# FFN of a cross-attention layer on one core: input and output products in one block with shared buffers, first operands of the output product loaded in the last step

## The chip, the cores and the metric

One core of a Trainium2 chip. The metric is the device time of the whole program in microseconds (us), the median of several executions.

## The reference

The layer is a cross-attention with a residual, followed by an FFN with a residual. `x` is [16, 112, 1024] float32, so there are 1792 tokens of width 1024. The part at issue is the FFN, cut here to what matters (`w1`, `w3` [3584, 1024], `w2` [1024, 3584] come as quantized values with one scale per 128x128 block; the quantization of the activations is undone at once and changes only rounding):

```
x = x + attention(layernorm(x), ctx)
h = silu(layernorm(x) @ w1.T) * (layernorm(x) @ w3.T)     # [1792, 3584]
out = x + h @ w2.T                                        # [1792, 1024]
```

## The kernel before

The program runs four stages, each a function of its own with its own `nc.Block()`: `queries`, `attention`, `mixing` (output projection, residual, second layer norm, transposed activations), `gate_up` (the two input products of the FFN) and `down` (the output product). At the end of a block all engines meet, and the buffers that a stage opened are given back. `stash` (12 x 1024 floats on each of 128 partitions) is the one buffer that outlives the stages.

Every float32 matrix product is made of three matmuls on operands split in a high part (rounded to `float32r`, made by ScalarE as a copy) and a low part (the rest, made by VectorE as `source - high` in `to_lo`, L90): high x high, high x low, low x high (L84, L85, L86 in `split_product`). Both FFN products are done by a Strassen-like scheme with 7 block products in place of 8.

**`gate_up`.** 56 steps `mi` (2 token halves x 28: 14 pairs of 128 hidden rows, `w1` and `w3` in turn). A step has 7 products `i` of 4 x 3 matmuls of 448 columns, counted by semaphore `prod`. ScalarE and VectorE split the next step's weights (`split_w`) while TensorE multiplies. VectorE adds the products (`add`, L1462), then forms `h = silu * up` in four blocks (`hidden`, L1467, in odd steps at i = 4, 5, 6: two at i = 4). GpSimd then forms four sums of the h blocks (`hidden_sums`, L1266 to L1274), and SyncE stores three h blocks and four sums (`store_h`, L1205, L1209) to `h_scr` in HBM. During the second half of the steps the kernel also prepares `w2`: VectorE transposes it (L1418), GpSimd forms four combinations (`down_sums`, L1282 to L1290), SyncE stores 3 + 4 blocks (`store_w2`, L1225, L1229) to `b_scr`. In the last step, mi = 55, the transposes of the last pair of `w2` are done at i = 0 to 3; there is nothing left to split for a next step. After the loop SyncE issues `store_w2(13)` and `store_h(27)`, and the block ends.

**`down`.** 49 tiles n = 7 i + t (7 block products i, 7 token tiles t of 128 tokens), each 14 x 3 matmuls of 512 columns into bank n % 8. The A operand (h, 128 x 1792 floats per tile, 896 KB) is loaded per tile into one of two slots, waits for its slot's split and is split whole (`AH`, `AL`). The B operand (w2, 14 pieces of 128 x 512 per i) is loaded in two halves of 7 pieces (1792 KB each) into one buffer of 7, and split piece by piece into a ring of 21. SyncE's queue in `down` is, in order: B half 0, A tile 0, B half 1, A tile 1, then the residual `y` (all 7 MB of it, 16 DMAs, L1637), then for each n: A tile n + 2, a B half at t = 0 and t = 6, and the stores of finished output tiles. VectorE's first output tile waits for the whole of `y`. VectorE and ScalarE do 7 B splits, then A tile 0, then the 7 other B splits, before they come to A tile 1. TensorE waits for A's low part at each tile, and in tile t = 0 for each piece of B.

The buffers of `down` are `y` [128, 2, 7, 1024], the rings `BH`, `BL`, and `AH`, `AL`; those of `gate_up` are `XH`, `XL`, `WH`, `WL`, `xT`, `t1`, `su`, `Sh`. They stand in the same memory one after the other, so nothing of `down` can be loaded before `gate_up` has ended, except into `stash`.

Of the kernel before, what the change touches and what calls it, by code (L numbers as in the profile page):

```python
# [21 lines left out]
def build_program(nc, x, ctx, wq, wk, wv, wo, w1, w1_scale, w3, w3_scale, w2, w2_scale, out):  # L22
# [7 lines left out]
    P = 128  # L30
    B, SQ, D = x.shape
# [26 lines left out]
    FB = 512  # L58
# [38 lines left out]
    with top:  # L97
# [1017 lines left out]
        def gate_up(xT):  # L1115
            with ExitStack() as st:
# [60 lines left out]
                def hcols(g):  # L1177
                    return slice(g * TB, (g + 1) * TB)

                with nc.Block() as block:  # L1180
                    @block.sync
                    def _(sp):
# [54 lines left out]
                        for mi in range(2 * NM):  # L1237
# [63 lines left out]
                    def _(act):  # L1301
# [63 lines left out]
                        for mi in range(2 * NM):  # L1365
                            P_, nxt = mi // 2, mi + 1 < 2 * NM
                            for i in range(7):
# [20 lines left out]
                                if i == 5 and mi >= NM and mi % 2 == 0:  # L1388
                                    scale_raw2((mi - NM) // 2)

                    @block.vector
                    def _(dve):
# [95 lines left out]
                        for mi in range(2 * NM):  # L1488
                            P_, up, nxt = mi // 2, mi % 2 == 1, mi + 1 < 2 * NM
                            for i in range(7):  # L1490
# [37 lines left out]
                                if i < 4 and mi >= NM and up:  # L1528
                                    make_w2T((mi - NM) // 2, i)

# [28 lines left out]

        def down():  # L1560
            with ExitStack() as st:
                def sb(name, shape, dt=f32):
                    return st.enter_context(nc.sbuf_tensor("d_" + name, shape, dt))

                def s_(name):
                    return sem("d_" + name)
                RING, HP = NP + NP // 2, NP // 2
                y = sb("y", [P, 2, MT, D])
                V = stash[:, 4:8, :].rearrange("p a (c n) -> p (a c) n", n=FB)
                BH, BL_ = sb("BH", [P, RING, FB], f32r), sb("BL", [P, RING, FB], f32r)  # L1570
                AH, AL = sb("AH", [P, 2, NP, P], f32r), sb("AL", [P, 2, NP, P], f32r)
                a_in = stash[:, 8:12, :].rearrange("p (e a) (c n) -> p e (a c) n", e=2, n=P)[:, :, 0:NP, :]
                b_in = stash[:, 0:4, :].rearrange("p a (c n) -> p (a c) n", n=FB)
                y_loaded = s_("y_loaded")
                a_loaded_ = [s_("a_loaded0"), s_("a_loaded1")]
                b_loaded = s_("b_loaded")
                a_hi, a_lo, b_hi, b_lo = s_("a_hi"), s_("a_lo"), s_("b_hi"), s_("b_lo")
                done, freed = s_("done"), s_("freed")
                v_done, c_done, out_ = s_("v_done"), s_("c_done"), s_("out")
                y_stored = s_("y_stored")  # L1580
                N = 7 * MT

                def part(r, c, t):
                    return y[:, r, t, c * FB:(c + 1) * FB]

                def rows(r, t):

                    out_rows, m = [], t * P
                    while m < (t + 1) * P:
                        n = min((t + 1) * P, (m // TB + 1) * TB) - m  # L1590
                        out_rows.append((m - t * P, n, m // TB * HALF + r * TB + m % TB))
                        m += n
                    return out_rows

                FINAL = {2: (0, 0), 4: (1, 1), 5: (1, 0), 6: (0, 1)}

                def ring(i, p):
                    return (NP * i + p) % RING

                with nc.Block() as block:  # L1600
                    @block.sync
                    def _(sp):
                        def load_b(i, h):

                            k = 2 * i + h
                            wait(sp, b_lo, HP * k)
                            sp.dma_start(b_in[:, 0:HP, :], b_scr[i, :, h * HP:(h + 1) * HP, :]
                                         ).then_inc(b_loaded, 16)

                        def load_a(n):  # L1610
                            i, t = n // MT, n % MT
                            wait(sp, a_lo, n - 1)
                            sp.dma_start(a_in[:, n % 2, :, :], h_scr[i, :, :, t * P:(t + 1) * P]
                                         ).then_inc(a_loaded_[n % 2], 16)

                        def store(i, t):
                            r, c = FINAL[i]
                            sp.wait_ge(out_, MT * sorted(FINAL).index(i) + t + 1)
                            for at, n, tok in rows(r, t):
                                sp.dma_start(of[tok:tok + n, c * FB:(c + 1) * FB],  # L1620
                                             part(r, c, t)[at:at + n, :]).then_inc(y_stored, 16)
                        of = out.rearrange("b q n -> (b q) n")
                        sp.wait_ge(b_stored, 112 * NP)
                        load_b(0, 0)
                        for stored in h_stored:
                            sp.wait_ge(stored, 48 * NP)
                        load_a(0)
                        sp.wait_ge(sh_stored, 64 * 2 * NP)
                        load_b(0, 1)
                        load_a(1)  # L1630
                        for stored in res_stored:
                            sp.wait_ge(stored, 16 * NT_TOK // 2)
                        n_res = 0
                        for t in range(MT):
                            for r in range(2):
                                for at, n, tok in rows(r, t):
                                    sp.dma_start(y[at:at + n, r, t, :], y_scr[tok:tok + n, :]  # L1637
                                                 ).then_inc(y_loaded, 16)
                                    n_res += 1
                        for n in range(N):  # L1640
                            i, t = n // MT, n % MT
                            if n + 2 < N:
                                load_a(n + 2)
                            if t in (0, MT - 1) and i + 1 < 7:
                                load_b(i + 1, 0 if t == 0 else 1)
                            if n and (n - 1) // MT in FINAL:
                                store((n - 1) // MT, (n - 1) % MT)
                        store(6, MT - 1)
                        sp.wait_ge(y_stored, 16 * sum(len(rows(r, t)) for r in range(2)
                                                      for t in range(MT)) * 2)  # L1650

                    def splits(eng, split_a, split_b, out_tile):
# [4 lines left out]
                        for n in range(N):  # L1657
                            i, t = n // MT, n % MT
                            if n + 1 < N:
                                split_a(n + 1)  # L1660
# [125 lines left out]
```

## Time and profile before

| | |
|---|---|
| median of 3 runs | 2568.43 us (2562.58 to 2568.75) |
| profiled execution | 2569.67 us, span 2567.7 us, mean granted TensorE clock 0.972 |
| TensorE busy | 2429.3 us (95% of the span), 12682 matmuls |
| VectorE, ScalarE, GpSimd busy | 1694.4, 980.1, 555.0 us |
| DMA | 408.02 MB, mean 159 GB/s |

The span is the time from the first to the last instruction of the profiled execution. Matmuls are pipelined, so "busy" of TensorE counts overlapping pieces; what tells is where it stood still and at which clock it ran. The clock column of the windows is 1.00 for 2.4 GHz and 0.50 for 1.2 GHz. "SPq" is a DMA issued from SyncE's queue.

### The profile page before, as it was taken

What the parts mean: (1) busy time and instruction counts of PE and PEld (TensorE: products, weight loads), DVE (VectorE), ACT (ScalarE), POOL (GpSimd) and SP (SyncE); (2) the same over time, 40 slices, a digit from 0 to 9 for tenths busy, and PEclk for the clock granted to TensorE, in tenths of its full rate; (3) what the DMA queues carried; (4) which work ended last, traced back from release to release, by engine and by line L of the source; (5) the groups of instructions that cost most, each with busy time, mean ns of one, the idle gap of its engine ahead of it and who ended that gap; (6) DMA issues with size and microseconds to landing.
All of it is one profiled execution on the core that took longest, in us unless ns stands there. A gap on an engine that the chain in (4) does not pass through costs nothing. (4 is left out here: it accounts for less than half of the span.)

```text
span 2567.7 us, 35357 instructions
## 1 busy us (share of the span) xinstructions
PE 2429.3 (95%) x12682; PEld 2073.0 (81%) x12682; DVE 1694.4 (66%) x2639; ACT 980.1 (38%) x1673; POOL 555.0 (22%) x305
## 2 busy tenths in 40 slices
PE   7998999999998799599999998999999949999999
PEld 6987877877884488499999987989898938888887
DVE  6425777777776444788888888788888734445442
ACT  3212445444444321544444444443344322332231
POOL 1000445445445300011111111233332210000000
PEclk9998999999998899799999999999999979999999
DMA  7535555555535435375566553677666595455552
GB/s 227 171 88 146 140 134 138 146 132 140 149 88 133 114 125 170 90 221 163 162 181 182 157 173 86 195 206 202 181 175 178 182 312 164 150 181 158 176 155 86
DMA packets 365224, 408.02 MB, mean 159 GB/s; under 512 B 125360, under 2 KB 323632, under 8 KB 356000
## 3 DMA queue, kind: packets, MB, share of 16 engines
q1 hardware_dynamic: 365088, 406.21, 54.7%
q8 instruction: 85, 1.39, 0.2%
q14 instruction: 51, 0.42, 0.1%
HBM read 252.99 MB, written 152.70 MB: 158 GB/s over the span
## 5 line engine op out<-in xcount | busy, mean ns | idle before, releaser
L84 PE MATMUL bank<-g_XH,g_WH 128*128 128x448 f32 x1568 | 580.7, 370 | 44.2 <-DVE g_su L1462 22.5
L85 PE MATMUL bank<-g_XL,g_WH 128*128 128x448 f32 x1568 | 578.5, 369 | 0.0
L86 PE MATMUL bank<-g_XH,g_WL 128*128 128x448 f32 x1568 | 578.3, 369 | 0.0
L1326 ACT ACTIVATE g_WH<-stash 128x512 fp32r<-128x512 f32 x392 | 241.6, 627 | 427.5 <-PE bank L86 249.2
L84 PEld LDWEIGHTS bank<-g_XH,g_WH 128*128 128x128 f32 x1568 | 296.5, 189 | 78.8 <-DVE g_WL L90 49.2
L696 DVE TENSOR_REDUCE a_nm<-bank 112x1 f32<-112x375 f32 x512 | 265.1, 531 | 116.8 <-PE bank L831 113.2
L90 DVE TENSOR_TENSOR g_WL<-stash,g_WH 128x512 fp32r<-128x512 f32 x392 | 283.8, 727 | 58.8 <-ACT g_WH L1326 49.7
L86 PEld LDWEIGHTS bank<-g_XH,g_WL 128*128 128x128 f32 x1568 | 296.4, 189 | 28.0
L85 PEld LDWEIGHTS bank<-g_XL,g_WH 128*128 128x128 f32 x1568 | 296.6, 189 | 27.6
L84 PE MATMUL bank<-d_BH,d_AH 128*128 128x512 f32 x686 | 269.4, 393 | 34.0 <-DVE d_AL L90 34.0
L800 ACT ACTIVATE a_pr<-bank 125x448 f32<-125x448 f32 x384 | 204.8, 545 | 207.4 <-PE bank L907 152.8
L85 PE MATMUL bank<-d_BL,d_AH 128*128 128x512 f32 x686 | 268.9, 392 | 0.0
L86 PE MATMUL bank<-d_BH,d_AL 128*128 128x512 f32 x686 | 268.7, 392 | 0.0
L649 POOL TENSOR_TENSOR a_prsum<-a_pr 125x1792 f32<-125x1792 f32 x32 | 129.3, 4042 | 364.0 <-ACT a_pr L800 364.0
L1673 ACT ACTIVATE d_AH<-stash 128x1792 fp32r<-128x1792 f32 x49 | 83.5, 1704 | 314.8 <-PE bank L86 292.2
L1462 DVE TENSOR_TENSOR g_su<-bank,g_su 128x448 f32<-128x448 f32 x280 | 170.6, 609 | 36.0 <-PE bank L86 35.9
L831 PE MATMUL bank<-a_kst,a_qst 96*112 96x376 f32 x512 | 183.1, 367 | 5.6 <-DVE a_nm L696 2.6
L84 PEld LDWEIGHTS bank<-d_BH,d_AH 128*128 128x128 f32 x686 | 130.1, 190 | 61.8 <-DVE d_AL L90 34.8
L85 PEld LDWEIGHTS bank<-d_BL,d_AH 128*128 128x128 f32 x686 | 130.1, 190 | 27.2
L86 PEld LDWEIGHTS bank<-d_BH,d_AL 128*128 128x128 f32 x686 | 130.0, 189 | 27.2
L907 PE MATMUL bank<-a_qst,a_kst 98*125 98x448 f32 x384 | 147.7, 389 | 2.9 <-ACT a_pr L800 2.6
L831 PEld LDWEIGHTS bank<-a_kst,a_qst 96*112 96x112 f32 x512 | 91.7, 179 | 69.3 <-DVE a_nm L696 32.7
(132 smaller groups left out, 4181.5 us busy)
## 6 DMA issues: line engine op xcount, KB each, us to landing
stash<-h_scratch SPq DMA_DIRECT2D x49, 896.0 KB, 5.7
stash<-in_L_ffn_w SPq DMA_DIRECT2D x168, 256.0 KB, 5.1
weight_scratch<-stash SPq DMA_DIRECT2D x28, 1024.0 KB, 7.7
stash<-weight_scratch SPq DMA_DIRECT2D x28, 1024.0 KB, 7.4
h_scratch<-g_Sh SPq DMA_DIRECT2D x112, 224.0 KB, 3.4
down_scratch<-xT SPq DMA_DIRECT2D x98, 256.0 KB, 3.0
stash<-down_scratch SPq DMA_DIRECT2D x14, 1792.0 KB, 8.8
stash<-in_ctx SPq DMA_DIRECT2D x48, 500.0 KB
```

What stands on the lines that cost most here:

```text
L84: pe.matmul(acc, lh, rh, start=first, stop=False, skip_group_check=onto)
L85: pe.matmul(acc, lh, rl, start=False, stop=False, skip_group_check=onto)
L86: return pe.matmul(acc, ll, rh, start=False, stop=last, skip_group_check=onto)
L90: return nc.vector.tensor_tensor(dst, src, hi.bitcast(f32), ALU.subtract)
L649: pool.tensor_tensor(prsum[:], pr[0:CK, :, 0, :], pr[0:CK, :, 1, :], ALU.add).then_inc(two_added, 1)
L696: nc.vector.tensor_reduce(nm[:, 1 - par, h:h + 1], s_bank[h % 2][0:SQ, 0:SK], AX.X, ALU.max, negate=True).then_inc(max_done, 1)
L800: nc.scalar.activation(pr[0:CK, r, c, :], st_bank[u % 2][0:CK, 0:J * SQ], ACT.Exp, scale=SCALE).then_inc(exp_done, 1)
L831: pe.matmul(s_bank[h % 2][0:SQ, 0:SKP], qst[0:96, 1 - par, g, j * SQ:(j + 1) * SQ], kst[0:96, 1 - par, g, :], start=True, stop=True).then_ ...
L907: pe.matmul(st_bank[u % 2][0:CK, 0:J * SQ], kst[0:98, par, g * R + r, c * CK:(c + 1) * CK], qst[0:98, par, g * R + r, :], start=True, stop ...
L1326: nc.scalar.activation(WH[:, i, :, :], w_source(mi, i), ACT.Copy).then_inc(w_hi, 1)
L1462: nc.vector.tensor_tensor(su[:, slot, :], acc[mi % 2][:, 0:TB], su[:, other, :], ALU.add).then_inc(summed, 1)
L1673: nc.scalar.activation(AH[:, n % 2, :, :], a_in[:, n % 2, :, :], ACT.Copy).then_inc(a_hi, 1)
```

## The change

`gate_up` and `down` become one function `ffn` with one block. Each engine's program for the output product (`down_sync`, `down_scalar`, `down_vector`, `down_tensor`) follows its program for the input products without a meeting point.

- The operands of the output product get the memory of the input products: the B ring (now 24 pieces) lies in `XH`/`XL`, the A slots in `WH`/`WL`, A tiles are loaded into a part of `hb` (in `stash`) and into `t1`, B pieces into `stash` (for i = 0 into 14 slots that the raw weights, `wT` and `S` held; from i = 1 on in chunks of 4 into 4 slots), the residual of r = 0 into `xT`, that of r = 1 into 14 free half rows of `stash`, `Sh` and `su`.
- In the last step (mi = 55) SyncE waits for the stores of the h blocks up to P_ = 26 and issues A tile 0; when the last weight split is done, B pieces 0 to 6, A tile 1, B pieces 7 to 11. Then `store_w2(13)`, a wait for it, B pieces 12 and 13, two residual tiles, `store_h(27)`, a wait for all h stores, and the tiles of the output product.
- In the last step ScalarE and VectorE split A tile 0 and B pieces 0, 1 at i = 4, pieces 2 to 4 at i = 5, pieces 5 to 11 at i = 6, behind that step's own additions and h blocks; pieces 12 and 13 come after the loop, then A tile 1.
- The residual is loaded tile by tile, in two column halves (32 DMAs in place of 16): r = 0 two tiles ahead, r = 1 from n = 3 on, one tile per n. An output tile waits for its own residual tile alone.
- From i = 1 on a chunk of B is loaded at t = 0, 2, 4, 6, each when all pieces of the one before it are split; pieces are split in the order `NEXT_B`.

```
-                RING, HP = NP + NP // 2, NP // 2
-                y = sb("y", [P, 2, MT, D])
-                BH, BL_ = sb("BH", [P, RING, FB], f32r), sb("BL", [P, RING, FB], f32r)
-                AH, AL = sb("AH", [P, 2, NP, P], f32r), sb("AL", [P, 2, NP, P], f32r)
+                RING, HP = 24, NP // 2
+                flat = [x[:, :, :, :].rearrange("p a k n -> p (a k n)") for x in (XH, XL)]
+                BH, BL_ = (f[:, 0:RING * FB].rearrange("p (s n) -> p s n", n=FB) for f in flat)
...
+                unit = stash[:, 0:8, :].rearrange("p a (c n) -> p (a c) n", n=FB)
+                BC = 4
...
+                def load_b(sp, i, c):
+                    p0, p1 = c * BC, min((c + 1) * BC, NP)
+                    sp.wait_ge(b_lo, NP * i + p0 if c else NP * i)
+                    sp.dma_start(unit[:, 0:p1 - p0, :], b_scr[i, :, p0:p1, :]).then_inc(d_b_loaded, 16)
+                FIRST_LOADS = ((0, HP), (HP, NP - 2), (NP - 2, NP))
+                def load_first_b(sp, k):
+                    p0, p1 = FIRST_LOADS[k]
+                    sp.dma_start(unit[:, b_slot(0, p0):b_slot(0, p1 - 1) + 1, :], b_scr[0, :, p0:p1, :]
+                                 ).then_inc(d_b_first[k], 16)
+                def load_a(sp, n):
+                    i, t = n // MT, n % MT
+                    wait(sp, a_lo, n - 1)
+                    sp.dma_start(a_in[n % 2], h_scr[i, :, :, t * P:(t + 1) * P]
+                                 ).then_inc(d_a_loaded[n % 2], 16)
+                def load_y(sp, r, t):
+                    for at, n, tok in rows(r, t):
+                        for c in range(2):
+                            sp.dma_start(part(r, c, t)[at:at + n, :], y_scr[tok:tok + n, c * FB:(c + 1) * FB]
+                                         ).then_inc(d_y_loaded[r][t], 16)
+                def down_sync(sp):
...
+                    for n in range(N):
+                        i, t = n // MT, n % MT
+                        if n + 2 < N:
+                            load_a(sp, n + 2)
+                        if t % 2 == 0 and i + 1 < 7:
+                            load_b(sp, i + 1, t // 2)
+                        if i == 0 and t + 2 < MT:
+                            load_y(sp, 0, t + 2)
+                        if n == 3:
+                            sp.wait_ge(b_lo, NP)
+                        if 3 <= n < 3 + MT:
+                            load_y(sp, 1, n - 3)
+                        if n and (n - 1) // MT in FINAL:
+                            store((n - 1) // MT, (n - 1) % MT)
...
+                FIRST_B = [range(0, 2), range(2, 5), range(5, NP - 2)]
+                NEXT_B = [range(*c) for c in ((0, 0), (0, 2), (2, 4), (4, 6), (6, 8), (8, 10), (10, NP))]
...
+                    dve_split_b(0, range(NP - 2, NP))
+                    for n in range(N):
+                        i, t = n // MT, n % MT
+                        if n + 1 < N:
+                            dve_split_a(n + 1)
+                        if i + 1 < 7:
+                            dve_split_b(i + 1, NEXT_B[t])
+                        out_tile(n)
...
                 with nc.Block() as block:
                     @block.sync
...
+                            if mi == 2 * NM - 1:
+                                sp.wait_ge(h_stored[0], 48 * NP)
+                                sp.wait_ge(h_stored[1], 48 * (NP - 1))
+                                sp.wait_ge(sh_stored, 64 * (2 * NP - 1))
+                                load_a(sp, 0)
+                                sp.wait_ge(w_lo, 7 * 2 * NM)
+                                sp.wait_ge(S_made, 4 * 2 * NM)
+                                sp.wait_ge(b_stored, 112 * (NP - 1))
+                                load_first_b(sp, 0)
+                                load_a(sp, 1)
+                                load_first_b(sp, 1)
...
                         store_w2(NP - 1)
+                        sp.wait_ge(b_stored, 112 * NP)
+                        load_first_b(sp, 2)
+                        load_y(sp, 0, 0)
+                        load_y(sp, 0, 1)
                         store_h(2 * NP - 1)
+                        for stored in h_stored:
+                            sp.wait_ge(stored, 48 * NP)
+                        sp.wait_ge(sh_stored, 64 * 2 * NP)
+                        sp.wait_ge(prod, 7 * 2 * NM)
+                        down_sync(sp)
...
                     @block.vector
...
                                 if i < 4 and mi >= NM and up:
                                     make_w2T((mi - NM) // 2, i)
+                                if mi == 2 * NM - 1 and i >= 4:
+                                    if i == 4:
+                                        dve_split_a(0)
+                                    dve_split_b(0, FIRST_B[i - 4])
+                        down_vector()
```

## Rows read from the trace of the kernel before

**Rows 1.** The page: the span in 40 equal slices, busy tenths of TensorE.

```profile
PE   7998999999998799599999998999999949999999
```

**Rows 2.** Timeline of TensorE around the change of stage (start us, us, ..., idle before).

```profile
2058.08 0.37 PE L86 MATMUL bank<-g_XH,g_WL 128*128 128x448 f32 x1
...
2079.64 0.80 PE L84 MATMUL bank<-d_BH,d_AH 128*128 128x512 f32 x1 [21.19 <-DVE d_AL L90]
...
2114.47 0.80 PE L84 MATMUL bank<-d_BH,d_AH 128*128 128x512 f32 x1 [12.77 <-DVE d_AL L90]
```

**Rows 3.** The chain that ended last, in order of time (start us, us, what).

```profile
2065.10 7.08 DMA stash<-down_scratch
...
2091.37 19.27 DMA stash<-h_scratch
```

**Rows 4.** Windows of 2 us: length, busy of PE, PEld, DVE, ACT, POOL, then clock, DMA share, GB/s.

```profile
2060.00:2062.00 2.00, 0.00 (x0) 0.00 (x0) 0.00 (x0) 0.00 (x0) 1.92 (x2) 0.90 0.71 256
...
2084.00:2086.00 2.00, 2.00 (x7) 1.57 (x6) 1.15 (x2) 1.81 (x4) 0.00 (x0) 0.63 1.20 312
...
2088.00:2090.00 2.00, 2.00 (x11) 1.65 (x10) 1.59 (x3) 1.54 (x1) 0.00 (x0) 1.00 1.02 410
...
2096.00:2098.00 2.00, 2.00 (x11) 1.65 (x10) 0.00 (x0) 0.00 (x0) 0.00 (x0) 1.00 1.05 242
```

**Rows 5.** Timelines: VectorE's output tiles in the steady stage, and the last instruction.

```profile
2393.28 1.29 DVE L1710 TENSOR_TENSOR d_y<-bank,d_y 128x512 f32<-128x512 f32 x2 [4.49 <-PE bank L86]
...
2402.80 1.29 DVE L1710 TENSOR_TENSOR d_y<-bank,d_y 128x512 f32<-128x512 f32 x2 [5.10 <-PE bank L86]
...
2564.64 0.69 DVE L1710 TENSOR_TENSOR d_y<-bank,d_y 128x512 f32<-128x512 f32 x1 [8.83 <-PE bank L86]
```

**Rows 6.** Timeline of VectorE in the last step and at the start of `down`.

```profile
2044.12 0.69 DVE L90 TENSOR_TENSOR g_WL<-stash,g_WH 128x512 fp32r<-128x512 f32 x1 [2.37 <-ACT g_WH L1326]
...
2053.53 0.62 DVE L1467 TENSOR_TENSOR stash<-bank,stash 128x448 f32<-128x448 f32 x1 [1.24 <-PE bank L86]
2054.07 1.46 DVE L1467 TENSOR_TENSOR stash<-g_su,stash 128x448 f32<-128x448 f32 x1
...
2059.14 0.62 DVE L1467 TENSOR_TENSOR stash<-g_su,stash 128x448 f32<-128x448 f32 x1
2072.86 4.30 DVE L90 TENSOR_TENSOR d_BL<-stash,d_BH 128x512 fp32r<-128x512 f32 x7 [13.09 <-ACT d_BH L1685]
2077.56 2.02 DVE L90 TENSOR_TENSOR d_AL<-stash,d_AH 128x1792 fp32r<-128x1792 f32 x1 [0.40 <-ACT d_AH L1673]
```

**Rows 7.** Timeline of GpSimd in the same stretch.

```profile
2053.74 1.30 POOL L1285 TENSOR_TENSOR xT<-xT 128x512 f32<-128x512 f32 x1
2055.00 1.68 POOL L1287 TENSOR_TENSOR xT<-xT 128x512 f32<-128x512 f32 x1
2056.63 1.30 POOL L1290 TENSOR_TENSOR xT<-xT 128x512 f32<-128x512 f32 x1
...
2063.22 1.13 POOL L1274 TENSOR_TENSOR g_Sh<-stash,g_Sh 128x448 f32<-128x448 f32 x1
```

**Rows 8.** Timeline of ScalarE, the first split of A.

```profile
2075.85 1.68 ACT L1673 ACTIVATE d_AH<-stash 128x1792 fp32r<-128x1792 f32 x1
```

**Rows 9.** Timeline of SyncE's queue (time of issue, not of landing).

```profile
2035.19 2.55 SPq L1229 DMA_DIRECT2D down_scratch<-xT  x4
2052.32 3.04 SPq L1225 DMA_DIRECT2D down_scratch<-xT  x3
```

**Rows 10.** The page's DMA issues: count, KB each, median us from issue to landing.

```profile
stash<-h_scratch SPq DMA_DIRECT2D x49, 896.0 KB, 5.7
stash<-in_L_ffn_w SPq DMA_DIRECT2D x168, 256.0 KB, 5.1
...
h_scratch<-g_Sh SPq DMA_DIRECT2D x112, 224.0 KB, 3.4
...
stash<-down_scratch SPq DMA_DIRECT2D x14, 1792.0 KB, 8.8
```

**Rows 11.** Windows of 2 us in earlier stages, where TensorE had short gaps.

```profile
1152.00:1154.00 2.00, 1.52 (x8) 1.42 (x9) 2.00 (x5) 1.05 (x2) 0.00 (x0) 1.00 0.96 401
...
828.00:830.00 2.00, 1.74 (x8) 0.90 (x4) 1.22 (x2) 1.52 (x3) 0.00 (x0) 0.50 0.42 115
```

More of the change, by code:

```diff
@@ L1113, in _, with ffn @@
                         transposes(NT_TOK - 1)
-        def gate_up(xT):
+        def ffn(xT):
             with ExitStack() as st:
@@ new lines, in ffn @@
+                unit = stash[:, 0:8, :].rearrange("p a (c n) -> p (a c) n", n=FB)
+                BC = 4
+                NC_B = -(-NP // BC)
+                V = unit[:, BC:BC + MT, :]
+                y_units = ([unit[:, k, :] for k in range(BC + MT, 16)]
+                           + [hb[:, 1, k, :] for k in range(4)]
+                           + [Sh[:, :, :].rearrange("p k n -> p (k n)")[:, k * FB:(k + 1) * FB] for k in range(3)]
+                           + [su[:, :, :].rearrange("p k n -> p (k n)")[:, k * FB:(k + 1) * FB] for k in range(2)])
@@ new lines, in ffn @@
+                d_y_loaded = [[sem(f"d_y_loaded{r}{t}") for t in range(MT)] for r in range(2)]
+                d_a_loaded = [sem("d_a_loaded0"), sem("d_a_loaded1")]
+                d_b_loaded, d_b_first = sem("d_b_loaded"), [sem(f"d_b_first{k}") for k in range(3)]
+                a_hi, a_lo, b_hi, b_lo = sem("d_a_hi"), sem("d_a_lo"), sem("d_b_hi"), sem("d_b_lo")
+                done, freed = sem("d_done"), sem("d_freed")
+                v_done, c_done, out_ = sem("d_v_done"), sem("d_c_done"), sem("d_out")
@@ new lines, in down_sync, with store @@
+                def down_sync(sp):
+                    of = out.rearrange("b q n -> (b q) n")
+                    def store(i, t):
+                        r, c = FINAL[i]
+                        sp.wait_ge(out_, MT * sorted(FINAL).index(i) + t + 1)
+                        for at, n, tok in rows(r, t):
+                            sp.dma_start(of[tok:tok + n, c * FB:(c + 1) * FB],
+                                         part(r, c, t)[at:at + n, :]).then_inc(y_stored, 16)
+                    for n in range(N):
[12 more added lines that the diff above has]
+                            store((n - 1) // MT, (n - 1) % MT)
+                    store(6, MT - 1)
+                    sp.wait_ge(y_stored, 16 * sum(len(rows(r, t)) for r in range(2)
+                                                  for t in range(MT)) * 2)
@@ new lines, in act_split_a, with act_split_b @@
+                def act_split_a(n):
+                    nc.scalar.wait_ge(d_a_loaded[n % 2], 16 * (n // 2 + 1))
+                    if n < 2:
+                        nc.scalar.wait_ge(prod, 7 * (2 * NM - 1) + (4 if n == 0 else 7))
+                    wait(nc.scalar, done, n - 1)
+                    nc.scalar.activation(AH[:, n % 2, :, :], a_in[n % 2], ACT.Copy).then_inc(a_hi, 1)
+                def act_split_b(i, ps):
+                    for p in ps:
+                        if i == 0:
+                            nc.scalar.wait_ge(d_b_first[0 if p < HP else 1 if p < NP - 2 else 2], 16)
+                        else:
+                            nc.scalar.wait_ge(d_b_loaded, 16 * (NC_B * (i - 1) + p // BC + 1))
+                        old = NP * i + p - RING
+                        if old >= 0:
+                            if old % NP == NP - 1:
+                                nc.scalar.wait_ge(done, MT * (old // NP + 1))
+                            else:
+                                nc.scalar.wait_ge(freed, (NP - 1) * (old // NP) + old % NP + 1)
+                        else:
+                            at = ring(i, p) * FB + FB - 1
+                            nc.scalar.wait_ge(prod, 7 * (2 * NM - 1) + at // (KH * TB) + 1)
+                        nc.scalar.activation(BH[:, ring(i, p), :], unit[:, b_slot(i, p), :], ACT.Copy
+                                             ).then_inc(b_hi, 1)
@@ L1755, in build_program @@
+                        down_tensor(pe)
         queries()
```

271 lines of the change are left out of this document (98 added, 173 removed).

## The prediction, made before the changed kernel was run

> **What bounds the kernel now.** I read the page's strip of 40 slices first: TensorE is at 8 or 9 tenths nearly everywhere in the FFN, with one slice of 4 near its three-quarter mark [rows 1]. The timeline of TensorE shows what is in that slice: the last input product ends at 2058.45 us (2058.08 + 0.37), the first output product starts after 21.19 us without a matmul, and tile 1 after another 12.77 us [rows 2]. The chain of waits tells why: a B half that is issued only when the old block has closed (7.08 us), and A tile 2 that takes 19.27 us because all of the residual and a B half are in front of it [rows 3]. To this comes the clock: it was 2.4 GHz until 2058.45, read 0.90 on average in 2060 to 2062, and came back within the window 2084 to 2086 (0.63 there, so at 2084 + 1.48 = 2085.5) [rows 4]. TensorE thus worked 5.9 us (2079.64 to 2085.5) at 1.2 GHz, which costs half of that, 2.9 us. The second gap I take at the same, 2.9. Sum: 21.2 + 12.8 + 2.9 + 2.9 = 39.8 us.
>
> A check by another way: in the steady stage output tiles follow each other at 2402.80 - 2393.28 = 9.52 us [rows 5], so 49 tiles take 466.5 us. From 2058.45 to the last output tile's addition at 2564.64 are 506.2 us. The difference is 39.7 us. All that the output stage loses is lost at its start; after that TensorE sets the pace. So at most 39.7 us are to be had.
>
> **Before the loop's end: the loads.** SyncE's queue is free from 2035.19 + 2.55 = 2037.7 until it stores w2 at 2052.32 [rows 9]. A tile 0 goes out at about 2038 and lands 5.7 us later [rows 10], at 2044. The B pieces wait for the last weight split, which ends at 2044.12 + 0.69 [rows 6]. B pieces 0 to 6 are the size that took 7.08 us alone [rows 3]: they land at about 2052. A tile 1 (0.92 MB) and five B pieces (1.31 MB) follow; together with the first (1.84 MB) 4.07 MB, at 242 to 410 GB/s (the two rates of long stretches under load [rows 4]) 10 to 17 us, so done between 2055 and 2062. I take 2058. The product stores of w2(13) (7 x 262 KB = 1.84 MB) queue behind them: done about 2063. Then B pieces 12, 13 are issued and land by 2068 (5.1 us for 256 KB [rows 10]). They are needed only at about 2073 (below), so a delay of 5 us is covered. These transfers lie beside matmuls that need none of them.
>
> The Trainium skill (DMA: Bandwidth & Descriptors, Where 436 GB/s comes from) puts the HBM side's limit for one core at about 358 GB/s. The row of 410 GB/s does not agree with it. By the page's 358 the 5.9 MB would take 16.5 us, by the row's 410 14.4 us: an estimate, and no change of the sum, since the pieces have their 5 us of cover.
>
> **The splits in the last step.** This is what I expect to set the new start, so VectorE's order is followed one by one. The unit prices: a B piece 4.30 / 7 = 0.614 us, an A tile 2.02 us [rows 6], 1.68 us on ScalarE [rows 8]. One thing more is in the rows: a VectorE operation on two SBUF sources takes turns with GpSimd. The h block at 2054.07 took 1.46 us, where the same one at 2059.14 took 0.62; it stood until GpSimd's operation ended at 2055.04 and GpSimd's next, 1.68 us instead of 1.30, stood for it [rows 6, 7]. The h block with a PSUM source at 2053.53 took 0.62 beside a GpSimd operation. The splits have two SBUF sources.
>
> At i = 4: ScalarE has A tile 0 at 2053.5 + 1.7 = 2055.2. VectorE is free at 2055.5, but must let GpSimd's operation end (2056.7), then works 2.0 us: 2058.7. GpSimd's last w2 sum follows (1.1 us), then B piece 0: 2060.4, piece 1: 2061.0. At i = 5 the step's addition and h block, 1.15 us: 2062.1; pieces 2 to 4: 2064.0. At i = 6 again 1.15: 2065.1, where it was at 2059.76 before (2059.14 + 0.62). Now GpSimd's four h sums start (1.13 each [rows 7]) and take turns with pieces 5 to 8: 1.75 us for each pair. Piece 8 is done at 2070.8 and 9 at 2072.5, if it also meets a sum, then 10 to 13 at 0.614 each: 2075.0; A tile 1: 2077.0.
>
> TensorE needs 0.68 us for a piece (9.52 / 14). It waits 1.9 us for piece 0, 1.0 for piece 2, 0.95 for piece 5 and 1.0 for each of 6 to 9, ends tile 0 at 2075.9 and starts tile 1 at 2077.0 (1.1). Sum 9.0 us lost, in place of 39.7.
>
> **A tile 2.** GpSimd's last h sum ends at about 2072 (2064.4 before), its store takes 3.4 us at the median [rows 10], so SyncE, which waits for all h stores before A tile 2, issues it at 2074 to 2075.5. It lands 5.7 us later, is split by 2084.5 (1.7 + 2.0), and tile 1 ends only at 2086.5. The cover is 2 us. Behind A tile 2 on SyncE's queue stand B's chunk 0, residual tile 2, A tile 3: none is late, as each has a tile's 9.5 us.
>
> **The residual.** It stood in front of A tile 2; now 0.5 to 1 MB are loaded per tile. The fullest tile (n = 4) has A 0.92, B 1.05, residual 1.05 to 1.57 MB: 3.0 to 3.5 MB, at 242 to 410 GB/s 7.4 to 14.6 us. Only three tiles are that full, and A tiles are issued two tiles ahead; I cost it at nothing, with 0 to 5 us for the range. Twice as many DMAs are issued for it, off the path of any engine but SyncE.
>
> **Chunks of 4 in the steady stage.** Chunk 3 can go only when pieces 10, 11 are split, 1.7 + 2.0 + 1.2 = about 5.1 us into tile t = 6. Behind it wait the splits of pieces 12, 13, the output tile's additions and the next A tile on ScalarE and VectorE, together about 5.7 us. The next tile but one needs that A at 19 us. So the load may take 8.2 us; 256 KB took 5.1 and 1792 KB 8.8 us [rows 10], and this is 512 KB, near the first. I take no cost; at 8.8 it is 6 times 0.6 = 3.6 us.
>
> **The clock.** Between 2058.45 and 2077 TensorE works 9.5 of 18.5 us. [...] So one fall is likelier than not. Its price: nothing, or 2.9 us as above, or 5.8 for two. I take 3.
>
> **The sum.** 2058.45 + 466.5 + 9.0 + 3.0 = 2537.0 for the last addition; the tail of the span is 2567.7 - 2564.64 = 3.1, the run's time 2.0 above its span: 2542.0 against 2569.67 for the profiled execution, 27.7 less. The median lies 1.2 below that execution: 2541.
>
> **Rivals.**
>
> 1. VectorE and GpSimd don't hinder each other here. For: the split at 2072.86 ran at 0.614 per piece, though with GpSimd idle. Then piece 0 is done at 2058, h at 2062.5, piece 11 at 2066.8, A tile 1 at 2070; TensorE loses 2.1 us and the clock stays. 2541 - 6.9 - 3 = 2531. Against it are rows 6 and 7. The Trainium skill (SBUF: State Buffer, Who interferes with whom) has a rule for this: a VectorE instruction with two SBUF inputs contends with a GpSimd instruction that reads SBUF; it gives no price for it, the rows above do. By that rule this rival is out, and the trace agrees (1.46 us against 0.62).
>
> 2. A tile 2 is late. It took 19.27 us with the residual ahead [rows 3]; now two residual tiles and B pieces stand before the h stores and may still be in flight. If it takes 19.3 from 2074.5, it is split at 2097.5, 11 us after tile 1's end, plus the clock 2.9: 2555. With half of that delay 2547. For: the cover is only 2 us. Against: 1 MB is ahead of it in place of 7.
>
> 3. Slower: the single buffer of 4 B pieces. Each of the six changes of i has its own stall if chunk 3 takes longer than 8.2 us. To give back 27 us each must be 4.6 us: from a landing of 12.8 us on. At 15 us: 6 x 6.8 = 41, 2582. Against: nothing of that size took this long but when the residual was in front.
>
> 4. The start gains nothing, because something holds tile 0 to the end of the h stores as before. TensorE's first tile waits for A, the pieces, and additions of step 54 that are long done, so I see no such wait; the time would be 2568.
>
> **Chances.** My forecast 0.65 (2535 to 2546), rival 1 0.10, rival 2 0.18, rival 3 0.04, rival 4 0.03. A measurement of this kernel tells from no change about 0.3%, 7.7 us. Faster than 2560.7: 0.92; the same: 0.04; slower: 0.04. The range takes in rival 1 at its lower end and most of rival 2: 2531 to 2552.
>
> **What would show it.** Right: TensorE's gap after the last input product about 2 us instead of 21.19; VectorE's splits of 1.2 to 1.8 us beside GpSimd's h sums; tile 0 stretched to 15 us or more, TensorE waiting for VectorE's B splits in it; no gap before tile 2; output tiles at 9.52 us from tile 2 on, at t = 0 too. Wrong: a gap before tile 2 that ends with a DMA (rival 2), regular gaps every seven tiles (rival 3), splits of 0.61 us beside GpSimd (rival 1), or a slower clock that lasts beyond tile 1.

## The result and the profile after

| | before | changed |
|---|---|---|
| median | 2565.51 us (4 runs, 2560.96 to 2568.75) | 2534.76 us (4 runs, 2530.68 to 2539.33) |
| profiled execution | 2569.67 us, span 2567.7 us | 2538.41 us, span 2536.6 us |

The ratio is 0.9881 with a 95% interval of [0.9862, 0.9901]: 1.2% faster, 30.8 us between the medians. The forecast was 2541, with a range of 2531 to 2552. A second series on another occasion gave 0.9872 [0.985, 0.9894].

The page's strip of TensorE no longer has the slice of 4 [rows 1]:

```profile
PE   7998999999999799599999998999999999999999
```

The timeline of TensorE after the last input product (2058.03 + 0.37 = 2058.40) shows a first gap of 1.93 us in place of 21.19 [rows 2], then short ones, and tile 1 at 2076.20 (start us, us, ..., [idle before]):

```profile
2058.03 0.37 PE L86 MATMUL bank<-g_XH,g_WL 128*128 128x448 f32 x1
2060.33 0.47 PE L84 MATMUL bank<-g_XH,g_WH 128*128 128x512 f32 x1 [1.93 <-DVE g_XL L90]
...
2062.63 0.50 PE L84 MATMUL bank<-g_XH,g_WH 128*128 128x512 f32 x1 [0.68 <-DVE g_XL L90]
...
2067.19 0.50 PE L84 MATMUL bank<-g_XH,g_WH 128*128 128x512 f32 x1 [0.59 <-DVE g_XL L90]
...
2076.20 0.50 PE L84 MATMUL bank<-g_XH,g_WH 128*128 128x512 f32 x1 [0.63 <-DVE g_WL L90]
```

Every gap up to tile 1 is ended by a split of VectorE. VectorE's timeline from i = 4 of the last step on, to be read against [rows 6], shows why:

```profile
2054.02 1.45 DVE L1704 TENSOR_TENSOR stash<-g_su,stash 128x448 f32<-128x448 f32 x1
2055.43 3.08 DVE L90 TENSOR_TENSOR g_WL<-stash,g_WH 128x1792 fp32r<-128x1792 f32 x1
2058.43 2.35 DVE L90 TENSOR_TENSOR g_XL<-stash,g_XH 128x512 fp32r<-128x512 f32 x2
...
2064.35 0.63 DVE L1704 TENSOR_TENSOR stash<-g_su,stash 128x448 f32<-128x448 f32 x1
2064.90 9.31 DVE L90 TENSOR_TENSOR g_XL<-stash,g_XH 128x512 fp32r<-128x512 f32 x9
2074.13 2.01 DVE L90 TENSOR_TENSOR g_WL<-g_t,g_WH 128x1792 fp32r<-128x1792 f32 x1
```

And GpSimd's in the same stretch, against [rows 7]:

```profile
2056.58 3.05 POOL L1522 TENSOR_TENSOR xT<-xT 128x512 f32<-128x512 f32 x1
2065.06 1.52 POOL L1498 TENSOR_TENSOR g_Sh<-stash 128x448 f32<-128x448 f32 x1 [5.43 <-DVE stash L1704]
...
2069.66 1.59 POOL L1506 TENSOR_TENSOR g_Sh<-stash,g_Sh 128x448 f32<-128x448 f32 x1
```

The split of A tile 0 took 3.08 us where it takes 2.02 alone: it stood until GpSimd's operation ended; GpSimd's next, which takes 1.30 alone, stood for it and took 3.05. The last nine pieces took 9.31 us, not 9 x 0.614 = 5.5.

The loads came when they were wanted. SyncE's queue (time of issue):

```profile
2037.20 0.59 SPq L1244 DMA_DIRECT2D stash<-h_scratch  x1
2044.78 0.33 SPq L1238 DMA_DIRECT2D stash<-down_scratch  x1
...
2063.31 0.32 SPq L1238 DMA_DIRECT2D stash<-down_scratch  x1
...
2075.05 0.53 SPq L1244 DMA_DIRECT2D stash<-h_scratch  x1
```

and ScalarE, which splits what has landed (B pieces 12, 13; A tile 1; A tile 2):

```profile
2067.52 1.15 ACT L1302 ACTIVATE g_XH<-stash 128x512 fp32r<-128x512 f32 x2 [5.33 <-DMA stash<-down_scratch]
2068.57 1.68 ACT L1285 ACTIVATE g_WH<-g_t 128x1792 fp32r<-128x1792 f32 x1
2080.78 1.70 ACT L1285 ACTIVATE g_WH<-stash 128x1792 fp32r<-128x1792 f32 x1 [10.53 <-DMA stash<-h_scratch]
```

A tile 2 landed at 2080.78, 5.7 us after its issue, in place of 19.27 [rows 3]. Its low part was ready at 2084.54; tile 1 ended at 2076.20 + 9.52 = 2085.72. TensorE's timeline shows no gap after tile 1.

**A measure that leaves the earlier stages out.** Executions of one kernel differ by up to 12 us (2560.8 to 2572.56 in nine runs of the kernel before), and the two traces of the changed kernel show that their difference arises before the last input product (see the end). So the experiments are compared by the time from the end of the last input product to the end of the span, each from one trace. It is 509.2 us in the kernel before (2567.7 - 2058.45), 478.2 in the changed one (2536.6 - 2058.40), and 478.4 when it was run again (2529.2 - 2050.78): 31.0 us less, and the two traces of the same kernel agree within 0.2.

### The profile page after: what moved, and what is told of

Its sections match the earlier page's. It is cut to its first block, busy times and chain, and to the rows that moved or that the text cites. A ratio compares the mean times of both kernels' runs of the same rounds, so it can differ in the third digit from the quotient of the medians.

```text
span 2536.6 us, 35412 instructions
## 1 busy us (share of the span) xinstructions
PE 2427.8 (96%) x12682; PEld 2071.4 (82%) x12682; DVE 1698.4 (67%) x2639; ACT 979.2 (39%) x1673; POOL 559.2 (22%) x305
## 4 chain that ended last, share of the span: by engine, by line
PE 44%; DVE 8%; DMA 3%; issue 2%; SPq 1%; ACT 1%; DVEq 0%; ACTq 0%
PE bank L84 15%; PE bank L85 14%; PE bank L86 14%; DMA stash<-weight_scratch 3%; DVE g_WL L90 2%; DVE g_XL L90 1%; DVE g_su L1699 1%; DVE xT L1655 1%; SPq L1431 1%; DVE stash L1667 1%; DVE stash L1666 1%; DVE stash L1669 1%; ACT stash L1548 0%; ACT g_WH L1558 0%; DVE stash L1643 0%
## 5 line engine op out<-in xcount | busy, mean ns | idle before, releaser
L84 PE MATMUL bank<-g_XH,g_WH 128*128 128x448 f32 (+1 forms) x2254 | 848.0, 376 | 51.8 <-DVE g_su L1699 24.2
L85 PE MATMUL bank<-g_XL,g_WH 128*128 128x448 f32 (+1 forms) x2254 | 845.0, 375 | 0.0
L86 PE MATMUL bank<-g_XH,g_WL 128*128 128x448 f32 (+1 forms) x2254 | 844.8, 375 | 0.0
L84 PEld LDWEIGHTS bank<-g_XH,g_WH 128*128 128x128 f32 x2254 | 425.2, 189 | 115.8 <-DVE g_WL L90 52.8
L86 PEld LDWEIGHTS bank<-g_XH,g_WL 128*128 128x128 f32 x2254 | 425.2, 189 | 54.1
L85 PEld LDWEIGHTS bank<-g_XL,g_WH 128*128 128x128 f32 x2254 | 425.4, 189 | 53.5
L90 DVE TENSOR_TENSOR g_WL<-stash,g_WH 128x512 fp32r<-128x512 f32 (+1 forms) x417 | 336.0, 809 | 77.4 <-ACT g_WH L1558 49.4
L645 POOL TENSOR_TENSOR a_prsum<-a_prsum,a_pr 125x1792 f32<-125x1792 f32 x32 | 128.7, 4022 | 1.8
L84 PE MATMUL bank<-a_w_h,a_cT_h 128*125 128x256 f32 x384 | 111.8, 291 | 0.0
L86 PE MATMUL bank<-a_w_h,a_cT_l 128*125 128x256 f32 x384 | 107.8, 281 | 0.0
```

Of the source, the lines that this page charges most:

```text
L84: pe.matmul(acc, lh, rh, start=first, stop=False, skip_group_check=onto)
L85: pe.matmul(acc, lh, rl, start=False, stop=False, skip_group_check=onto)
L86: return pe.matmul(acc, ll, rh, start=False, stop=last, skip_group_check=onto)
L90: return nc.vector.tensor_tensor(dst, src, hi.bitcast(f32), ALU.subtract)
L645: pool.tensor_tensor(prsum[:], prsum[:], pr[0:CK, :, 2, :], ALU.add).then_inc(all_added, 1)
```

## The experiments

**The early loads alone undone (e2_late_loads).** One block and the residual tile by tile stay; the loads of i = 0 follow the stores, the splits follow the loop.

```diff
-                            if mi == 2 * NM - 1:
-                                ...
-                                load_a(sp, 0)
-                                ...
-                                load_first_b(sp, 0)
-                                load_a(sp, 1)
-                                load_first_b(sp, 1)
                         store_w2(NP - 1)
+                        store_h(2 * NP - 1)
                         sp.wait_ge(b_stored, 112 * NP)
+                        load_first_b(sp, 0)
+                        for stored in h_stored:
+                            sp.wait_ge(stored, 48 * NP)
+                        load_a(sp, 0)
+                        sp.wait_ge(sh_stored, 64 * 2 * NP)
+                        load_first_b(sp, 1)
+                        load_a(sp, 1)
                         load_first_b(sp, 2)
...
-                                if mi == 2 * NM - 1 and i >= 4:
-                                    if i == 4:
-                                        dve_split_a(0)
-                                    dve_split_b(0, FIRST_B[i - 4])
+                        dve_split_a(0)
+                        dve_split_b(0, range(0, NP - 2))
                         down_vector()
```

> One block and the residual tile by tile are kept; the early part is undone: A tiles 0, 1 and all B pieces of i = 0 are loaded after the stores of w2 and h, and split after the loop. My theory (the early loads removed the first gap): B pieces 0 to 6 land at about 2072, A tile 0 at 2074.5, piece 0 is split at about 2079; TensorE stands still for about 21 us after the last input product, at 1.2 GHz for some 5 us after that; no gap before tile 2. In place of the 8.3 us lost by the changed kernel 24: about 2550 us. Rival (the gain is the residual's, or the meeting of the engines at the block's end, and the loads would be hidden either way): within 3 us of the changed kernel, 2535.

Measured: 2548.08 us (ratio to before 0.9935 [0.9911, 0.9959]); from the last input product to the end 492.7 us, 14.5 more than the changed kernel. TensorE has one gap of 21.14 us and none before tile 2. So the two parts of the change are worth 14.5 us (loads and splits brought forward) and 16.5 us (509.2 - 492.7, the rest: residual tile by tile, one block). The second adds up from the traces: 12.77 us of standing still [rows 2], 2.6 us for the half clock behind it (2114.47 to 2119.6), and 1.1 us because the half clock behind the first gap lasted 3.6 us in e2 and not 5.8. The clock came back within these windows, the first of the kernel before, the second of e2:

```profile
2118.00:2120.00 2.00, 2.00 (x7) 1.57 (x6) 0.87 (x3) 1.83 (x2) 0.00 (x0) 0.59 1.18 283
```

```profile
2078.00:2080.00 2.00, 2.00 (x6) 1.52 (x5) 2.00 (x4) 2.00 (x5) 0.00 (x0) 0.55 1.04 389
```

The first gap is as long as before (21.14 and 21.19 us): one block without the early loads did not shorten it.

**The early splits alone undone (e3_late_splits).** The loads stay early; the splits follow the loop, as in the last lines of the diff above.

> The early loads are kept; ScalarE and VectorE split A tile 0 and B pieces 0 to 11 after the loop, not between the last step's additions. My theory (the sum of VectorE's work up to A tile 1, with its turns with GpSimd, sets tile 1): the h blocks are ready at 2059.8, GpSimd's h sums start there and take turns with the first pieces; the first output product starts at about 2063.5 (3 us later than in the changed kernel), but A tile 1 is ready at 2076.3, as in the changed kernel: no change of tile 1 by that, and 0 to 3 us from a fall of the clock in the 5 us gap: 2535 to 2539. Rival (what is split within the last step is gained in full): tile 1 later by the 3 us and more, 2541 with the clock.

Measured: 2532.82 us (0.9871 [0.9846, 0.9896]); to the end 478.3 us, the same as the changed kernel. And yet the first output product came 6.11 us after the last input product, not 1.93, and the clock fell. Windows of 2 us (busy of PE, PEld, DVE, ACT, POOL, then clock, DMA share, GB/s):

```profile
2054.00:2056.00 2.00, 0.00 (x0) 0.00 (x0) 2.00 (x1) 2.00 (x5) 1.92 (x2) 0.90 0.83 318
2056.00:2058.00 2.00, 0.00 (x0) 0.01 (x1) 2.00 (x3) 2.00 (x5) 2.00 (x2) 0.50 0.03 12
...
2060.00:2062.00 2.00, 2.00 (x5) 1.16 (x4) 2.00 (x3) 0.95 (x3) 0.42 (x1) 0.50 1.13 332
2062.00:2064.00 2.00, 2.00 (x9) 1.61 (x8) 2.00 (x5) 1.92 (x2) 0.00 (x0) 0.89 0.73 243
```

Neither cost anything: A tile 1 was ready 17.6 us after the last input product (2067.52 + 2.02 - 2051.92) as in the changed kernel (2074.13 + 2.01 - 2058.40 = 17.7), and TensorE, which worked its first 4.4 us at 1.2 GHz, came to tile 1 at 2069.97, 0.4 us after it was ready and 18.0 us after the last input product (17.8 in the changed kernel):

```profile
2053.91 2.41 DVE L90 TENSOR_TENSOR g_WL<-stash,g_WH 128x1792 fp32r<-128x1792 f32 x1 [0.68 <-ACT g_WH L1285]
2056.25 11.34 DVE L90 TENSOR_TENSOR g_XL<-stash,g_XH 128x512 fp32r<-128x512 f32 x14
2067.52 2.02 DVE L90 TENSOR_TENSOR g_WL<-g_t,g_WH 128x1792 fp32r<-128x1792 f32 x1
```

The splits inside the last step gain nothing by themselves, so the 14.5 us above are those of the early loads. VectorE's and GpSimd's timelines of e3 show why:

```profile
2049.52 0.62 DVE L1697 TENSOR_TENSOR g_su<-bank,g_su 128x448 f32<-128x448 f32 x1 [0.39 <-PE bank L86]
2050.18 0.63 DVE L1702 TENSOR_TENSOR stash<-g_su,stash 128x448 f32<-128x448 f32 x1
2051.95 0.62 DVE L1697 TENSOR_TENSOR g_su<-bank,g_su 128x448 f32<-128x448 f32 x1 [1.15 <-PE bank L86]
...
2050.24 1.71 POOL L1522 TENSOR_TENSOR xT<-xT 128x512 f32<-128x512 f32 x1
```

VectorE stood idle 2.2 us in e3 (0.39, 1.15 and 0.68) where the changed kernel has it split. But A tile 0 and the 14 pieces took 2.41 + 11.34 = 13.8 us there, and 3.08 + 2.35 + 1.89 + 9.31 = 16.6 in the changed kernel: its early splits meet GpSimd's last two w2 sums, which in e3 were done at 2051.95, before the splits. What is gained by filling the idle time is paid in turns. That the two cancel is a matter of this kernel's numbers.

**The residual in front of A tile 2 again (e1_residual_first).**

```diff
+                    for t in range(2, MT):
+                        load_y(sp, 0, t)
                     for n in range(N):
                         ...
-                        if i == 0 and t + 2 < MT:
-                            load_y(sp, 0, t + 2)
```

> The other residual tiles of r = 0 (2 to 6, 2.6 MB) are issued in one go in front of A tile 2, in place of one per tile. My theory (what stood in front of A tile 2 made the second gap): A tile 2 lands at 2086 to 2091, its low part is ready at 2090 to 2095, where tile 1 ends at 2085.7: a gap of 4 to 9 us before tile 2 and the clock behind it: 2539 to 2547. Rival (transfers overlap, the residual was not what made A late): no gap, 2535.

Measured: 2541.25 us (0.991 [0.9887, 0.9932]); to the end 489.0 us, 10.7 more. A gap of 7.89 us before tile 2, ended by A tile 2's split, and half clock for 5.3 us behind it (2086.49 to about 2091.8), which costs half of that; the two make up 10.5 of the 10.7 us. SyncE's queue shows that the issue itself was pushed back by 6.25 us, before the transfer:

```profile
2068.03 6.25 SPq L1250 DMA_DIRECT2D xT<-y_scratch  x12
2074.33 0.56 SPq L1244 DMA_DIRECT2D stash<-h_scratch  x1
```

The transfer was slower too: 8.3 us from issue to landing in place of 5.7. Five residual tiles of the 14 bring back more than half of the old second gap (7.89 of 12.77 us).

**More work for GpSimd (e7_sums_twice).** Four additions in front of the last four h sums.

```diff
+                            if P_ == 2 * NP - 1:
+                                for k in range(4):
+                                    wait(pool, extra, k)
+                                    pool.tensor_tensor(Sh[:, 3, :], h[:, H12, :], h[:, H22, :], ALU.add
+                                                       ).then_inc(extra, 1)
+                                pool.wait_ge(extra, 4)
```

> GpSimd does four more additions of h blocks before its four h sums of the last pair (they are overwritten, the output stays the same). My theory (VectorE's operations on two SBUF sources take turns with GpSimd): four more B pieces take 1.55 us in place of 0.61, so A tile 1 is ready and tile 1 starts 3.8 us later, at 2080.0; the h sums end at about 2077, A tile 2 is ready at about 2091, 1 to 2 us after tile 1's end. Together some 6 us longer than the changed kernel. Rival (no turns, the pieces are slow for another reason): tile 1 at 2076.2 as before, only A tile 2 later.

Measured: one execution, 2541.59 us; to the end 482.2 us, 4.0 more. Tile 1 starts 21.7 us after the last input product in place of 17.8: 3.9 later, 3.8 was expected. The nine pieces took 13.11 us, 3.8 more than 9.31, at 0.95 for each addition:

```profile
2064.27 13.11 DVE L90 TENSOR_TENSOR g_XL<-stash,g_XH 128x512 fp32r<-128x512 f32 x9
```

The extra 1 to 2 us before tile 2 did not come: A tile 2 was ready at 2088.26, tile 1 ended at 2088.89. Between the end of GpSimd's last sum and the issue of A tile 2 lay 2.1 us (2076.83 to 2078.89) in place of 3.8 (2071.25 to 2075.05).

**A tile 2 in front of the last h stores (e4_a2_first), GpSimd's last sums behind A tile 1's split (e5_sums_late), both (e6_both).** In e4 the wait for the h sums' stores moves to where their first reader is near:

```diff
                         load_first_b(sp, 2)
+                        load_a(sp, 2)
                         load_y(sp, 0, 0)
                         load_y(sp, 0, 1)
-                        store_h(2 * NP - 1)
+                        store_h_blocks(2 * NP - 1)
+                        store_h_sums(2 * NP - 1)
                         for stored in h_stored:
                             sp.wait_ge(stored, 48 * NP)
-                        sp.wait_ge(sh_stored, 64 * 2 * NP)
...
                         if n == 3:
                             sp.wait_ge(b_lo, NP)
+                            sp.wait_ge(sh_stored, 64 * 2 * NP)
```

e5 is the changed kernel with one line more; e6 has both, and `store_h_sums` is called at n = 1 of the output product's loop.

```diff
+                        pool.wait_ge(a_lo, 2)
                         hidden_sums(2 * NP - 1)
```

> A tile 2 is loaded before the last h blocks are stored (its tokens belong to the first half, whose h is stored long before). My theory (A tile 2 had a cover of 1 us and was hidden): the first output product, tile 1 and tile 2 start as in the changed kernel; A tile 2 lands by about 2071 and is split as soon as its slot is free; time 2535, within 1 us in the trace. Rival (loading behind the h stores costs something already): faster by 1 us or more.

> GpSimd waits with the four h sums of the last pair until A tile 1 is split; SyncE's order is as in the changed kernel. My theory: without turns VectorE's pieces 5 to 9 take 0.61 us, A tile 1 is ready at 2072.3 (3.9 us earlier), but the h sums' stores land at 2080.5, A tile 2 is ready at 2090, 8 us after tile 1's end, the clock falls: 4 to 7 us longer than the changed kernel, 2539 to 2542. Rival (no turns): tile 1 as before at 2076.2, a gap before tile 2 of 4 us.

> Both: A tile 2 is loaded before the last h stores, GpSimd's last h sums wait for A tile 1's split, and SyncE stores them during tile 1 (they are needed from tile 7 on). My theory (turns with GpSimd cost VectorE's splits 3.9 us, and nothing else then holds tile 2): tile 1 starts at 2072.3, tile 2 at 2081.8, the output stage ends 3.9 us earlier than in the changed kernel: 2531. Rival (TensorE or a load sets the pace of tile 0): within 1 us of it.

Measured, from the last input product to the end: e4 478.5 us (the changed kernel 478.2 and 478.4), e5 484.6, e6 474.6. The times: 2538.27 and 2544.78 us (one execution each), e6 2534.67 us (0.9875 [0.9857, 0.9894]) beside 2531.61 us (0.9872 [0.985, 0.9894]) of the changed kernel in the same series.

In e4 nothing moved: A tile 2 had been hidden. In e5, by one line, the nine pieces took 5.50 us and tile 1 came 14.4 us after the last input product, 3.4 earlier, but then TensorE stood 6.57 us for A tile 2 and fell to half clock: earlier splits, lost again behind the h stores. In e6 the pieces run at 0.61 us as well and A tile 2 is there:

```profile
2058.61 5.50 DVE L90 TENSOR_TENSOR g_XL<-stash,g_XH 128x512 fp32r<-128x512 f32 x9
2064.03 2.02 DVE L90 TENSOR_TENSOR g_WL<-g_t,g_WH 128x1792 fp32r<-128x1792 f32 x1
```

The gain of 3.7 us (3.9 was expected) stands in one trace of the stage. The timed series don't show it: the median of e6 is even 3.1 us above the changed kernel's, and the intervals of the two ratios overlap; the variation of the earlier stages is larger than 0.15%.

**The last chunk of B later (e8_chunk_late).**

```diff
+                        if t == 6 and i + 1 < 7:
+                            sp.wait_ge(done, n + 1)
                         if t % 2 == 0 and i + 1 < 7:
                             load_b(sp, i + 1, t // 2)
```

> The last chunk of B of each of the six changes of i (pieces 12, 13) is loaded only when tile t = 6 has ended, 4.4 us later than its predecessor's splits would allow. My theory (the single buffer of four pieces has a cover of 5 us at each change of i: A of the next tile but one is ready 5.1 us before it is needed): no gap on TensorE after tile 1, and from the last input product to the end 478.3 us as in the changed kernel. Rival (the single buffer is at its limit): gaps at t = 0 or 1 of each i, six times 1 to 4 us: 484 to 502 us.

Measured: one execution, 2528.64 us; to the end 478.7 us, no gap of TensorE after tile 1. At the second change of i the chunk was issued when the tile ended (2190.22) and landed 3.7 us later, and A's low part was ready at 2199.12, 0.4 us before the next tile's first matmul at 2199.55:

```profile
2193.90 1.15 ACT L1304 ACTIVATE g_XH<-stash 128x512 fp32r<-128x512 f32 x2 [10.39 <-DMA stash<-down_scratch]
...
2194.96 1.69 ACT L1287 ACTIVATE g_WH<-g_t 128x1792 fp32r<-128x1792 f32 x1
```

At the fourth change A was ready only at 2330.87 + 2.02 = 2332.89, and the tile's first matmul came 0.34 us after the one before it, not 0.23:

```profile
2332.60 0.39 PE L86 MATMUL bank<-g_XH,g_WL 128*128 128x512 f32 x1
2332.94 0.50 PE L84 MATMUL bank<-g_XH,g_WH 128*128 128x512 f32 x1
```

So a delay of 4.4 us just fits.

## Why the prediction was right

**What there was to gain.** 39.7 us were lost at the start of the output product. 31.0 of them went. Of the two parts that the chain of [rows 3] named, the first is shown by e2 (14.5 us); the second is what e2 leaves, 16.5, and e1 shows its cause, since 10.7 us come back with five residual tiles alone. One reading in the prediction is wrong: the 12.77 us of [rows 2] stood before tile 2, not before tile 1. Tile 0 had started at 2079.64 and lasted 9.52 + 2.9 us, tile 1 another 9.52, which ends at 2101.6; and it was A tile 2 that landed late. The sum does not depend on it.

**The loads in the last step.** Forecast and trace: A tile 0 issued at 2038 and 2037.20; pieces 12, 13 issued at about 2063 and 2063.31, landed by 2068 and at 2067.52. VectorE came to piece 12 at about 2073, so 5.5 us of cover remained. The 5.9 MB that the sum counts went out and landed from 2044.78 to 2063.31, at 319 GB/s on average, between the two bounds. That the transfers set this issue and not GpSimd's last w2 sum, which ended 1.2 us after the last input product, is seen in e3: there the sum ended with it (2051.95), and the issue came no earlier, 5.4 us after the last input product in place of 4.9.

**VectorE sets the new start.** This step carried the number, and it was right: first output product at 2060.4 forecast, 2060.33 measured; tile 1 at 2077.0 and 2076.20. TensorE lost 2076.20 - 2067.92 = 8.3 us, 9.0 were forecast. The 0.7 us lie in the size of the turns: a piece and a GpSimd sum together took 1.55 us, not 1.75; a sum holds VectorE up for 0.95 us of the 1.13 that it takes alone. That the turns are the cause is shown from both sides: four sums more cost 3.8 us of VectorE's time (e7), four fewer give 3.8 back (9.31 to 5.50 in e5 and e6). The order in which I followed the operations put the gaps where they came. The first had the forecast length (1.93 us); the others were 0.59 to 0.69 us in the trace, not 0.95 to 1.1. e3 qualifies the working: the splits inside the last step, which I followed one by one, have no price of their own here, because the turns with the w2 sums take what the filled idle time gives.

**The clock.** I put 3.0 us on it and it cost nothing. In the profiled execution the windows read 1.00 all through tile 0, where TensorE was busy 1.11 to 2.00 of each 2 us:

```profile
2064.00:2066.00 2.00, 1.31 (x7) 0.77 (x6) 1.97 (x4) 0.00 (x0) 0.94 (x1) 1.00 0.88 184
...
2070.00:2072.00 2.00, 1.11 (x4) 0.63 (x5) 2.00 (x3) 0.26 (x1) 1.25 (x1) 1.00 1.06 404
```

This is the mis-sized term, and not because the fall was unlikely: the clock stayed in this trace, its repetition and e7, and fell early in tile 0 in e1, e4, e5, e6 and e8, which run the same program up to there. In e8 it fell after 2.08 us of standing still and 1 us of work:

```profile
2050.00:2052.00 2.00, 1.82 (x6) 1.16 (x6) 1.97 (x5) 1.89 (x4) 0.00 (x0) 0.80 0.92 353
2052.00:2054.00 2.00, 1.72 (x5) 1.22 (x5) 2.00 (x4) 0.00 (x0) 0.00 (x0) 0.50 0.06 23
```

Why it stays in some executions and falls in others is not shown. The fall cost next to nothing: e8 took 478.7 us to the end and e4 478.5, against 478.2 and 478.4 without one, since TensorE in tile 0 waits for VectorE anyway. e3, with 6.11 us of standing still and 4.4 us at half clock, is at the limit: it took 478.3 us, with no wait left at tile 1. The half clock costs half its length where TensorE has everything at hand afterwards, as behind tile 2's gap in e1.

**The sum.** Forecast for the profiled execution 2542.0, measured 2538.41: 3.0 of the 3.6 us are the clock, 0.7 the turns. The medians lie lower in both kernels (2565.51 and 2534.76), within the variation described below; that the forecast median (2541) was off by 6.2 us and not by 3.6 is no fault or merit of its working.

**A tile 2.** Forecast issue 2074 to 2075.5, measured 2075.05; ready at 2084.54 with 1.2 us of cover, 2 forecast; when it was run again the cover was 0.6 us (2077.68 against 2068.72 + 9.52 = 2078.24). Rival 2 (it is late) was thus near, and that it stayed away is partly luck: e5 shows it, with 6.57 us and the clock, and e4 that there was nothing to be had from it alone.

**The residual tile by tile, the chunks of four.** No gap of TensorE is left after tile 1, so both cost nothing, as put. At t = 6 the 512 KB chunk was issued at 2195.83 and landed at 2199.57, 3.7 us (allowed: 8.2). Delayed by 4.4 us it still cost at most 0.5 us over six changes (e8): rival 3 is out. The cover is 4.4 us at the tightest change, a little less than the 5.1 expected.

**Rival 1** (no turns) would have had tile 1 at 2070. Rows of the trace, e5, e6 and e7 are against it. **Rival 4** (no gain) fell with the result.

What stays open: e7 expected 1 to 2 us before tile 2 that did not come. Most of it is the 1.7 us by which SyncE issued A tile 2 sooner after GpSimd's last sum. The h blocks' stores were then long issued (by 2066.96), so SyncE may have had less to wait for; I did not test this.

## What to carry to other kernels

When a stage change costs a gap, write down for the next stage's first tile each engine's operations one by one: what bounds the new start can be no longer the load but the engine that prepares the operands, here VectorE, and then what counts is the time at which its last piece is ready: the sum of its work, its turns with GpSimd and its idle time. Moving pieces into idle time gains nothing if they meet more of GpSimd's operations there, as here. If VectorE's operations on two SBUF sources fall beside GpSimd's, add about one GpSimd operation to each (here 0.95 us of the 1.13), and look whether that GpSimd work has a reader soon; delaying it pays only if no load waits for its store. And put large transfers with a late reader behind small ones with an early reader on the same queue: 2.6 MB in front of one tile cost 10.7 us.

## What the runs showed that was not expected

**Two rates of the same matmuls at the same clock.** In the window from 1160 to 1480 us, deep in the first half of the input products, TensorE's busy time is the whole window and the granted clock is 1.00 in every trace. Yet some executions do 1550 matmuls there and others 1580 or 1581: 0.2065 us against 0.2024 for each. The first line is the changed kernel's profiled execution, the second, a trace of its own, the same kernel run again:

```profile
1160.00:1480.00 320.00, 320.00 (x1550) 290.62 (x1549) 275.37 (x407) 150.04 (x256) 53.75 (x36) 1.00 0.59 168
```

```profile
1160.00:1480.00 320.00, 320.00 (x1581) 296.61 (x1580) 280.00 (x416) 155.05 (x262) 53.82 (x36) 1.00 0.59 171
```

Over these 320 us that is 6.3 us, most of the difference of the ends of the last input product (2058.40 and 2050.78). Matmuls missing from a record don't explain it: VectorE and ScalarE are ahead by the same 2% (416 operations against 407, 262 against 256). Of the eleven traces six have the slow rate (before, changed, e2, e4, e5, e7) and five the fast one (changed again, e1, e3, e6, e8); no experiment changes anything that runs up to there. It is a large part of why executions of one kernel lie so far apart, and why changes of 4 us had to be read from the stage's own length. From 1650 to 1950 us, in the second half of the input products, the two traces are alike again (1443 and 1447 matmuls). What sets the rate was not tried.

**The turns are of whole operations.** A GpSimd operation and a VectorE operation on two SBUF sources alternate one by one here, and each waits for nearly the whole of the other, at both lengths seen: GpSimd's w2 sum took 3.05 us (1.30 alone) behind VectorE's 2.02 us split of A, and its h sums 1.48 to 1.60 (1.13 alone) beside pieces of 0.61.
